# Gated cross attention and a quantized gated FFN on one core: seam between the two halves rewritten, out projections in two banks, weight passes spread over the steps, last two tiles' up products together

## The chip, the cores and the metric

One core of one Trainium2 chip. The metric is the device time of one execution in microseconds, the median over several runs.

## The reference

Inputs: `x` and `ctx` (8 x 256 x 512), attention weights with a latent width of 128, FFN weights w1, w2 (2048 x 512) and w3 (512 x 2048). For each of the 8 batches:

```
xn     = layernorm(x, axis=-1)                       # 256 rows of 512
theta  = theta_w @ ctx + theta_b                     # 128 x 512
phi    = phi_w @ xn + phi_b ;  g = g_w @ xn + g_b
p      = softmax(theta.T @ phi, axis=-1)             # 512 x 512
t_x    = g @ p.T                                     # 128 x 512
h      = relu((t_x - mean) * rsqrt(var + 1e-5) * gamma + beta)   # mean, var over all of t_x
x      = x + tanh(g_xattn) * (out_w @ h + out_b + ctx)
```

Then, row by row of all 2048 rows (16 tiles of 128 rows):

```
y      = layernorm(x)
bitlinear(a, w) = quant127(rmsnorm(a)) @ ternary(w).T      # per-row scale, one scale per weight
h      = silu(bitlinear(y, w1)) * bitlinear(y, w2)
x      = x + tanh(g_ffn) * bitlinear(h, w3)
```

## The kernel before, in words

The program is written engine by engine, each engine's instructions in a fixed order, with semaphores between them. It has two halves.

**Attention**, a loop of eight steps `i` (one batch each). On TensorE (PE) a step is `theta(i)`, `out_proj(i-3, 0)`, `phi(i)`, `mean_mm(i-2)`, `out_proj(i-3, 1)`, `g(i)`, then four rounds of `scores(i, c)`, `turn_p(i-1, c)` (transposes of the probabilities) and `values(i-1, c)`. So three batches are in flight. VectorE (DVE) takes the row maxima, the low halves of theta and phi, the layer norm of `t_x`, and adds each out projection to `x` (`add_out`, L675). ScalarE (ACT) copies products out of the banks, takes the exponentials and, in slots `slot(i, 0..6)` of each step, the **weight passes** of the FFN's ternary quantization: `weight_abs` (L435, `M` in the table) and `weight_sign` (L440, `S`), 128x1024 each, 8 of each kind per weight; a table `weight_work` says which pass stands in which slot. GpSimd (POOL) normalises the probabilities (L307), rounds the weights (L321) and takes all inverse roots (L283).

Both halves of an out projection go to one bank (`b_at`, bank 6), so `out_proj(i, 1)` waits until `add_out(i, 0)` has read it:

```
if 2 * i + o >= 1:
    pe.wait_ge(x2_ready, 2 * i + o)
```

**FFN**, a loop over 16 tiles `t`: `up(t, c)` for four column groups, each 4 matmuls of 128x512 with w1 and 4 with w2 into a pair of banks (L1023), SiLU on ACT (L501), `hmul` on DVE (L733) writes the hidden tile; `absmax` (L738) and `square` (L507) per half tile, `root_h` and `quant_h` on POOL (L374, L380) quantize it; a DMA transpose (L246) turns it; `down(t)` is 16 matmuls of 128x512 (L1042). PE's order is `up(t, 0..3)`, `down(t-2)`. Before a pair of tiles the input is prepared: `row_stats` and `prep_mean` (DVE), `center` (ACT), `prep_root` (POOL), `prep_max` and `prep_scale` (DVE), `prep_quant` (POOL), `turn_x` (a DMA transpose).

**The seam** is the stretch between the halves: the last batch's transposes and values, batches 5 to 7's layer norms and out projections, mixed by hand with tiles 0 and 1. There `prep_root(2)` stands on POOL between `root_h(1)` and `quant_h(1)`, and `row_stats(2)` on DVE in tile 2.

**The tail**: for the last tile the hidden tile is turned by 16 PE transposes (L1117) with copies on ACT and DVE (L583, L902), between `down(14)` and `down(15)`; before them PE runs `down(13)`, `down(14)`.

The start: 14 warm-up matmuls (L1048, two passes each), then `theta(0)`, once `ctx` of batch 0 has landed as one load.

Of the kernel before, what the change touches and what calls it, by code (L numbers as in the profile page):

```python
# [12 lines left out]
P = 128  # L13
# [21 lines left out]
def gated_cross_attention_bitffn(nc, x, ctx_in, pack_a, pack_b, pack_c, w1t, w2t, w3t, out):  # L35
# [22 lines left out]
    with ExitStack() as ctx:  # L58
# [33 lines left out]
        identb = sb("identb", [P, P], BF16)  # L92
# [35 lines left out]
        hT = [prob[:, k, 2:4].rearrange("p a t -> p (a t)").bitcast(BF16) for k in range(2)]  # L128
        xo = [stage[:, 4 * WP + k * T:4 * WP + (k + 1) * T] for k in range(2)]
# [3 lines left out]
        b_th, b_ph, b_g, b_tx, b_at, b_st = banks[0], banks[1], banks[2], banks[3], banks[6], banks[7]  # L133
# [14 lines left out]
        (pa_loaded, pb_loaded, pc_loaded, xa_loaded, ident_made, gates_ready, xvar_ready, xrstd_ready, xn_ready, cb_made,  # L148
# [4 lines left out]
            "pa_loaded", "pb_loaded", "pc_loaded", "xa_loaded", "ident_made", "gates_ready", "xvar_ready",  # L153
# [11 lines left out]
         tail_t_done, tail_T_ready) = [sem(n) for n in (  # L165
            "fvar_ready", "y_ready", "fr_ready", "fqs_ready", "xq_ready", "s12_ready",
            "up1_done", "up2_done", "sil_done", "hm_done", "sq_done", "hms_ready", "hr_ready", "qs_ready", "hq_ready",
            "dn_done", "xo_ready", "tail_a_ready", "tail_q_ready", "tail_t_done", "tail_T_ready")]
        tail_q1_ready, tail_T1_ready = sem("tail_q1_ready"), sem("tail_T1_ready")
# [14 lines left out]
        def _(sp):  # L184
# [19 lines left out]
            load_c(0)  # L204
# [51 lines left out]
            for t in range(1, NT):  # L256
# [12 lines left out]
        def _(pool):  # L269
# [882 lines left out]
```

## Time and profile before

| | us |
|---|---|
| median of 3 runs | 312.59 (312.37 to 313.79) |
| profiled execution, its own time | 312.92 |
| its span in the trace | 309.9 |
| PE busy | 298.2 (96%) |
| DVE / ACT / POOL busy | 240.3 / 196.2 / 195.9 |

The span runs from the first to the last instruction that the profile shows; 3.0 us of the execution's own time lie around it. Busy times of matmuls are modelled and overlap, so a busy PE can still be waiting a little. The start-to-start distance of two matmuls is the measure of what one costs.

### The profile page before, as it was taken

How to read it: one execution, taken by the hardware profiler on the slowest of the kernel's cores; microseconds unless marked ns; L12 is line 12 of the kernel's file. 1: busy time of each engine (PE TensorE's matmuls, PEld its weight loads, DVE VectorE, ACT ScalarE, POOL GpSimd, SP SyncE). 2: the span in 40 equal slices, each digit the busy share in tenths (PEclk: the TensorE clock that was granted, in tenths of full speed). 3: DMA queues.
4: the chain of work that ended last, by engine and by line, in shares of the span. 5: the costliest groups of instructions: out<-in, count | busy, mean ns of one | idle time of the engine just before them, and what ended most of it. 6: DMA issues, size and time to landing. Idle time of an engine off the chain costs nothing.

```text
span 309.9 us, 4392 instructions
## 1 busy us (share of the span) xinstructions
PE 298.2 (96%) x1345; PEld 161.4 (52%) x1362; DVE 240.3 (78%) x515; ACT 196.2 (63%) x343; POOL 195.9 (63%) x297
## 2 busy tenths in 40 slices
PE   8999999999999999999897999999999999999994
PEld 8766657575757665444343444444444444444451
DVE  3897878796969795877698798787976896768572
ACT  1498999789999837665953644736465546355430
POOL 3360959584949177683458878778686786655510
PEclk9999999999999999999999999999999999999999
DMA  7999953545020001010305433354234561642242
GB/s 261 418 414 413 384 211 139 203 135 205 0 69 0 0 6 30 1 36 1 68 2 102 103 63 91 85 122 117 53 83 102 71 119 52 138 102 48 54 102 102
DMA packets 50518, 36.45 MB, mean 118 GB/s; under 512 B 40896, under 2 KB 41024, under 8 KB 49472
## 3 DMA queue, kind: packets, MB, share of 16 engines
q1 hardware_dynamic: 50352, 36.05, 39.8%
q10 hardware_dynamic: 144, 0.13, 0.3%
q8 instruction: 10, 0.16, 0.2%
q14 instruction: 12, 0.10, 0.1%
HBM read 22.02 MB, written 4.19 MB: 85 GB/s over the span
## 4 chain that ended last, share of the span: by engine, by line
PE 70%; ACT 15%; DVE 9%; issue 4%; POOL 0%; DVEq 0%; ACTq 0%; POOLq 0%
PE bank L1023 30%; PE bank L1042 17%; ACT wq L435 5%; PE bank L969 4%; PE bank L951 4%; ACT prob L482 4%; PE bank L938 3%; PE bank L982 3%; PE bank L962 3%; ACT probT L478 2%; PE bank L1048 2%; PE bank L920 2%; DVE stage L733 1%; DVE x L675 1%; PE bank L930 1%
## 5 line engine op out<-in xcount | busy, mean ns | idle before, releaser
L1023 PE MATMUL bank<-wq,stage 128*128 128x512 bf16 x498 | 113.2, 379 | 3.4 <-DVE stage L733 2.7
L1023 PEld LDWEIGHTS bank<-wq,stage 128*128 128x128 bf16 x512 | 49.8, 98 | 65.9 <-DVE stage L733 5.2
L733 DVE SCALAR_TENSOR_TENSOR stage<-bank,s,stage 128x512 f32<-128x512 f32 x64 | 47.7, 745 | 30.7 <-PE bank L1023 20.6
L507 ACT ACTIVATE xn<-stage 128x1024 f32<-128x1024 f32 x32 | 33.8, 1057 | 47.8 <-DVE stage L733 47.8
L1042 PE MATMUL bank<-wq,prob 128*128 128x512 bf16 x253 | 57.4, 379 | 1.1 <-ACT prob L583 1.0
L501 ACT ACTIVATE stage<-bank,s 128x512 f32<-128x512 f32 x64 | 42.7, 680 | 21.3 <-PE bank L1023 19.2
L374 POOL TENSOR_SCALAR stage<-stage,hsc 128x1024 f32<-128x1024 f32 x30 | 33.4, 1122 | 21.5 <-DVE hsc L753 21.5
L307 POOL TENSOR_SCALAR prob<-prob,rsum 128x512 f32<-128x512 f32 x32 | 21.6, 693 | 35.8 <-DVE rsum L639 35.8
L1042 PEld LDWEIGHTS bank<-wq,prob 128*128 128x128 bf16 x256 | 25.0, 98 | 30.9 <-issue 0.9
L738 DVE TENSOR_REDUCE m<-stage 128x1 f32<-128x1024 f32 x32 | 38.9, 1216 | 0.8
L951 PE MATMUL bank<-ph,th 128*128 128x512 f32 x96 | 36.0, 488 | 0.0
L969 PE MATMUL bank<-probT,gs 128*128 128x512 f32 x64 | 32.9, 599 | 0.9 <-ACT probT L478 0.5
L380 POOL TENSOR_SCALAR prob<-stage 128x1024 bf16<-128x1024 f32 x30 | 30.9, 1046 | 0.0
L633 DVE TENSOR_REDUCE nmax<-bank 128x1 f32<-128x512 f32 x32 | 21.9, 690 | 10.8 <-PE bank L951 10.8
L321 POOL TENSOR_SCALAR stage<-stage,winv 128x1024 f32<-128x1024 f32 x24 | 29.2, 1230 | 0.4
L440 ACT ACTIVATE wq<-stage,neground 128x1024 bf16<-128x1024 f32 x24 | 26.9, 1150 | 0.0
L478 ACT COPY probT<-bank 128x512 f32<-128x512 f32 x32 | 18.7, 590 | 12.7 <-PE bank L962 12.7
L951 PEld LDWEIGHTS bank<-ph,th 128*128 128x128 f32 x96 | 17.5, 189 | 11.7 <-issue 10.0
L482 ACT ACTIVATE prob<-bank,nmax 128x512 f32<-128x512 f32 x32 | 22.3, 697 | 1.7 <-DVE nmax L633 1.7
L435 ACT ACTIVATE wq<-stage 128x1024 bf16<-128x1024 f32 x21 | 22.2, 1058 | 0.0
L962 PE MATMUL bank<-ident,prob 128*128 128x128 f32 x128 | 19.3, 275 | 0.0
L982 PE MATMUL bank<-hn,pc 128*128 128x512 f32 x32 | 17.3, 623 | 1.5 <-DVE x L675 1.1
(107 smaller groups left out, 421.7 us busy)
## 6 DMA issues: line engine op xcount, KB each, us to landing
c_sb<-ctx_in_dram SPq DMA_DIRECT2D x8, 512.0 KB, 3.9
stage<-w1t_dram SPq DMA_DIRECT2D x4, 1024.0 KB, 12.3
stage<-w2t_dram SPq DMA_DIRECT2D x4, 1024.0 KB, 14.7
stage<-w3t_dram SPq DMA_DIRECT2D x4, 1024.0 KB, 5.4
out_dram<-stage SPq DMA_DIRECT2D x16, 256.0 KB, 2.3
x<-x_dram SPq DMA_DIRECT2D x7, 512.0 KB, 11.7
pc<-pack_c_dram SPq DMA_DIRECT2D x1, 640.0 KB, 16.6
x<-x_dram SPq DMA_DIRECT2D x2, 256.0 KB, 3.6
```

The source lines that it names most:

```text
L374: link.inc(G.tensor_scalar(part, part, hsc[:, 5:6], ROUND, ALU.mult, ALU.add))
L380: G.tensor_scalar(hq[t % 2][:, lo:hi], h[:, lo:hi], -ROUND, 1.0, ALU.add, ALU.mult).then_inc(hq_ready, 1)
L435: A.activation(wq[:, at:at + WP], piece(k, p), ACT.Abs, accum_out=wsum[:, k, p:p + 1]).then_inc(wabs_done, 1)
L482: A.activation(prob[:, i % 2, c], b_sc(i, c)[:, :], ACT.Exp, bias=nmax[:, c:c + 1], accum_out=esum[:, c:c + 1]).then_inc(exp_done, 1)
L501: A.activation(sil[n % 3], up_banks(n)[0][:, :], ACT.Silu, scale=s12[:, u % 2, 0, k:k + 1]).then_inc(sil_done, 1)
L507: A.activation(junk, h_sb[t % 2][:, half * HF:(half + 1) * HF], ACT.Square, accum_out=ssq[:, half:half + 1]).then_inc(sq_done, 1)
L733: V.scalar_tensor_tensor(h_sb[k][:, c * 512:(c + 1) * 512], up_banks(n)[1][:, :], s12[:, u % 2, 1, k:k + 1], sil[n % 3], ALU.mult, ALU.mul ...
L738: link.inc(V.tensor_reduce(m2[:, half:half + 1], h_sb[t % 2][:, half * HF:(half + 1) * HF], AX_X, ALU.max, apply_absolute_value=True))
L951: last = mm(b_sc(i, c)[:, :], th[:, a, c * P:(c + 1) * P], ph[:, b], start=n == 0, stop=n == 2)
L969: last = mm(b_tx[:, :], gs[:, i % 2, c * P:(c + 1) * P], probT[:, c % 2], start=c == 0, stop=c == TC - 1)
L1023: last = mm(bank[:, :], turned[:, row:row + P], wq[:, at:at + 512], start=q == 0, stop=q == KI - 1)
L1042: last = mm(b_dn[t % 2][:, :], hT[t % 2][:, q * P:(q + 1) * P], wq[:, at:at + T], start=q == 0, stop=q == KF - 1)
```

## The change

What it does:

- **Start.** 9 warm-up matmuls for 14; batch 0's `ctx` loaded as two halves, waited for one by one by `theta(0)`; `phi(0)` waits for each half of `xn` by itself.
- **Weight passes.** The table has other entries (below): slot 4, before `g_copy`, is empty in steps 1 to 4, passes move to slots 5 and 6 and to later steps. In step 2 the weight's total, its scale and `mean_mm(0)` move behind `phi(2)` and `g(2)`.
- **Out projections.** The two halves go to two banks, `b_out(i, o)`; `out_proj(i, 1)` waits for `add_out(i-1, 1)` and no more for `add_out(i, 0)`. As bank 5 is also a transpose bank, `turn_p(i, 1)` waits for `add_out(i-2, 0)`.
- **Seam.** POOL normalises two of the last batch's four probability tiles, ACT the other two. `silu(0, 0)` stands between the copies of the last batch. Tile pair 2 is prepared inside the seam: `row_stats`, `prep_mean`, `center`, `prep_max` earlier, `prep_root(2)` behind `quant_h(0)`. The last weight signs, `hidden_scale`, `add_out`, `tx_gamma` and `out_proj(7, 1)` change places.
- **prep_scale.** Its operations on two columns become operations on one column each, and the scale that `prep_quant` waits for is written before the others.
- **Tail.** PE runs `up(14)`, `up(15)`, then `down(12)`, `down(13)`, `down(14)`, and tile 15's down product in two halves of 256 columns in two banks. Tile 15 is turned by DMA transposes, its last half tile is squared and maximised in two pieces, and its output is stored in two halves, the second from ACT's queue. The PE transposes and their copies are gone.

The diff, cut to its core:

```diff
+        def b_out(i, o):
+            if i < B - 2:
+                return (banks[5], banks[6])[o]
+            return ((banks[2], banks[6]), (banks[6], banks[2]))[i - (B - 2)][o]
...
-            load_c(0)
+            sp.dma_start(c_sb[:, 0, 0], c_v[0][:, 0]).then_inc(ca_loaded, 16)
+            sp.dma_start(c_sb[:, 0, 1], c_v[0][:, 1]).then_inc(c_loaded[0], 16)
...
-            normalise(B - 1)
+            normalise(B - 1, 2)
             tx_root(B - 2)
             rounds(2, 2, 4)
             prep_quant(1)
             rounds(2, 4, 8)
+            root_h(0)
             tx_root(B - 1)
-            root_h(0)
             quant_h(0)
+            prep_root(2)
             for t in range(2, NT):
                 root_h(t - 1)
-                if t == 2:
-                    prep_root(2)
                 quant_h(t - 1)
...
-                1: (None, (M, 0, 3), None, (M, 0, 4), (M, 0, 5), (M, 0, 6), (M, 0, 7)),
-                2: ((M, 1, 0), (M, 1, 1), (M, 1, 2), (M, 1, 3), (M, 1, 4), (M, 1, 5), (M, 1, 6)),
-                3: ((M, 1, 7), (S, 0, 0), (S, 0, 1), (S, 0, 2), (S, 0, 3), None, None),
-                4: ((S, 0, 4), (S, 0, 5), (S, 0, 6), (S, 0, 7), (M, 2, 0), (M, 2, 1), (M, 2, 2)),
-                5: ((S, 1, 0), (S, 1, 1), (S, 1, 2), (S, 1, 3), (M, 2, 3), (M, 2, 4), (M, 2, 5)),
-                6: ((S, 1, 4), (S, 1, 5), (M, 2, 6), (M, 2, 7), None, (S, 1, 6), (S, 1, 7)),
-                7: (None,) * 7,
+                1: (None, (M, 0, 3), None, (M, 0, 4), None, (M, 0, 5), (M, 0, 6)),
+                2: ((M, 0, 7), (M, 1, 0), (M, 1, 1), (M, 1, 2), None, (M, 1, 3), (M, 1, 4)),
+                3: ((M, 1, 5), (M, 1, 6), (M, 1, 7), (S, 0, 0), None, (S, 0, 1), (S, 0, 2)),
+                4: ((S, 0, 3), (S, 0, 4), (S, 0, 5), (S, 0, 6), None, (S, 0, 7), (M, 2, 0)),
+                5: ((S, 1, 0), (S, 1, 1), (S, 1, 2), (S, 1, 3), (M, 2, 1), (M, 2, 2), (M, 2, 3)),
+                6: ((S, 1, 4), (S, 1, 5), (M, 2, 4), (M, 2, 5), None, (M, 2, 6), (M, 2, 7)),
+                7: ((S, 1, 6), None, (S, 1, 7), None, None, None, None),
...
+            act.wait_ge(rsum_ready, B)
+            for c in (2, 3):
+                A.activation(prob[:, 1, c], prob[:, 1, c], ACT.Copy, scale=rsum[:, c:c + 1]).then_inc(pnorm_ready, 1)
             p_copy(B - 1, 0)
             p_copy(B - 1, 1)
+            silu(0, 0)
             p_copy(B - 1, 2)
...
-                link.inc(V.tensor_tensor(fsc[:, 8], fsc[:, 6], fsc[:, 7], ALU.mult))
-                link.wait(dve)
-                link.inc(V.tensor_scalar(fsc[:, 9], fsc[:, 8], QUANT_EPS, None, ALU.max))
+                for k in range(2):
+                    link.inc(V.tensor_scalar(fsc[:, 9, k:k + 1], fsc[:, 6, k:k + 1], fsc[:, 7, k:k + 1], QUANT_EPS,
+                                             ALU.mult, ALU.max))
...
             tx_norm(B - 2)
             prep_scale(1)
+            row_stats(2, 0)
+            row_stats(2, 1)
+            prep_mean(2)
             hmul(0, 1)
...
             def turn_p(i, c):
+                if c == 1 and i >= 2:
+                    pe.wait_ge(x2_ready, 2 * (i - 2) + 1)
...
-                if 2 * i + o >= 1:
-                    pe.wait_ge(x2_ready, 2 * i + o)
+                if o == 0 and i == B - 2:
+                    pe.wait_ge(exp_done, 4 * B)
+                elif i >= 1 and (o, i) != (1, B - 1):
+                    pe.wait_ge(x2_ready, 2 * i if o == 1 or i == B - 1 else 2 * i - 1)
...
-            for _ in range(14):
+            for _ in range(9):
                 mm(b_st[:, 0:P], avg[:, :], avg[:, :], start=True, stop=True)
...
             out_proj(B - 1, 0)
+            out_proj(B - 1, 1)
             for t in range(2, NT):
                 for c in range(FC):
                     up(t, c)
-                    if t == 2 and c == 0:
-                        out_proj(B - 1, 1)
-                down(t - 2)
-            down(NT - 2)
-            for half in range(2):
-                pe.wait_ge((tail_q_ready, tail_q1_ready)[half], 1)
...
-            down(NT - 1)
+                if t < NT - 2:
+                    down(t - 2)
+            for t in range(NT - 4, NT - 1):
+                down(t)
+            down_last()
```

ACT at the end of attention step 7 and the begin of the seam: `hn<-hn` is a relu, `stage<-x,fmv` the centering of tile pair 1, `prob,esum<-bank` an exponential, `probT<-bank` the copies of turned probabilities, `stage<-bank,s` a SiLU. Before:

```order
L482 ACTIVATE prob,esum<-bank,nmax 128x512
L501 ACT_TABLE_LOAD
L501 ACTIVATE stage<-bank,s 128x512
L440 ACTIVATE wq<-stage,neground 128x1024
L478 COPY probT<-bank 128x512 x4
L474 ACTIVATE hn<-hn 128x512
```

and now:

```order
L516 ACTIVATE prob,esum<-bank,nmax 128x512
L584 ACTIVATE prob<-prob,rsum 128x512 x2
L512 COPY probT<-bank 128x512 x2
L535 ACT_TABLE_LOAD
L535 ACTIVATE stage<-bank,s 128x512
L512 COPY probT<-bank 128x512 x2
L474 ACTIVATE wq<-stage,neground 128x1024
L508 ACTIVATE hn<-hn 128x512
```

Two normalising passes are new ahead of the first copies; the table load and the first SiLU have moved from before all four copies to between the second and the third; the weight sign has moved behind the copies.

POOL in the seam, from the root of tile 0's hidden tile (`hsc`) on; `fsc` is the preparation of tile pair 2, `stage<-stage,hsc` and `prob<-stage` are the two halves of `quant_h`. Before:

```order
L283 TENSOR_TENSOR hsc<-hsc,neghalf 128x1
L331 TENSOR_SCALAR fsc<-fmv 128x2
L283 TENSOR_TENSOR fsc<-fsc,neghalf 128x2
L335 TENSOR_TENSOR fsc<-fmv,fsc 128x2
L337 TENSOR_TENSOR fsc<-fsc 128x2
L339 TENSOR_SCALAR fsc<-fsc 128x2
L283 TENSOR_TENSOR fsc<-fsc,neghalf 128x2
L343 TENSOR_TENSOR fsc<-fsc 128x2
L374 TENSOR_SCALAR stage<-stage,hsc 128x1024 x2
```

and now:

```order
L415 TENSOR_SCALAR prob<-stage 128x1024 x2
L353 TENSOR_SCALAR fsc<-fmv 128x2
L305 TENSOR_TENSOR fsc<-fsc,neghalf 128x2
L357 TENSOR_TENSOR fsc<-fmv,fsc 128x2
L359 TENSOR_TENSOR fsc<-fsc 128x2
L361 TENSOR_SCALAR fsc<-fsc 128x2
L305 TENSOR_TENSOR fsc<-fsc,neghalf 128x2
L365 TENSOR_TENSOR fsc<-fsc 128x2
L380 TENSOR_TENSOR hsc<-ssq 128x1
L382 TENSOR_SCALAR hsc<-hsc 128x1
L305 TENSOR_TENSOR hsc<-hsc,neghalf 128x1
L409 TENSOR_SCALAR stage<-stage,hsc 128x1024 x2
```

The seven `fsc` operations stood between tile 1's root and its quantization; now they stand behind tile 0's quantization and ahead of tile 1's root.

PE in the tail, from the up products of tile 14 on. Before:

```order
L1023 MATMUL bank<-wq,stage 128x512 x32
L1042 MATMUL bank<-wq,prob 128x512 x16
L1023 MATMUL bank<-wq,stage 128x512 x32
L1042 MATMUL bank<-wq,prob 128x512 x32
L1117 MATMUL bank<-identb,prob 128x128 x16
L1042 MATMUL bank<-wq,prob 128x512 x16
```

and now:

```order
L1115 MATMUL bank<-wq,stage 128x512 x64
L1133 MATMUL bank<-wq,prob 128x512 x32
L1133 MATMUL bank<-wq,gs 128x512 x16
L1146 MATMUL bank<-wq,probT 128x256 x32
```

The 16 transposes are gone, and three down products instead of one and a half stand between the last up product and the last down product.

## Rows read from the trace of the kernel before

**Rows 1.** The page: busy times, and the shares of the chain that ended last.

```profile
PE 298.2 (96%) x1345; PEld 161.4 (52%) x1362; DVE 240.3 (78%) x515; ACT 196.2 (63%) x343; POOL 195.9 (63%) x297
...
PE 70%; ACT 15%; DVE 9%; issue 4%; POOL 0%; DVEq 0%; ACTq 0%; POOLq 0%
```

**Rows 2.** Windows, in us: length, busy of PE, PEld, DVE, ACT, POOL, PEclk, DMA, GB/s.

```profile
121.90:170.00 48.10, 43.91 (x186) 19.90 (x189) 38.00 (x82) 30.86 (x47) 30.48 (x44) 1.00 0.17 33
170.00:294.40 124.40, 123.77 (x566) 56.44 (x577) 97.53 (x208) 66.89 (x110) 89.11 (x138) 1.00 0.41 88
```

**Rows 3.** Chain of waits, one down product of the FFN: start, length, line.

```profile
190.86 3.45 PE bank L1042 x16
```

**Rows 4.** Timeline, the start: start, busy, instruction, [idle before it, ended by].

```profile
0.98 5.98 PE L1048 MATMUL bank<-avg 128*128 128x128 f32 x28 [0.98 <-POOL avg L272]
...
10.23 1.95 PE L938 MATMUL bank<-pb,xn 128*128 128x128 f32 x16
...
8.67 0.69 DVE L603 BATCH_NORM_STATS2 xst<-x 128x6 f32<-128x512 f32 x1 [0.98 <-DMA x<-x_dram]
```

**Rows 5.** Timeline, attention steps 1 and 2: an ACT weight pass, and PE where it waited.

```profile
20.13 1.04 ACT L435 ACTIVATE wq<-stage 128x1024 bf16<-128x1024 f32 x1
...
22.28 1.12 PE L969 MATMUL bank<-probT,gs 128*128 128x512 f32 x2 [0.46 <-ACT probT L478]
...
33.09 0.35 PE L990 MATMUL bank<-tsc,avg 128*128 128x1 f32 x2 [0.48 <-DVE winv L694]
```

**Rows 6.** Timeline of PE: mean and second out projection in steps 3, 4 and 7.

```profile
47.90 0.28 PE L990 MATMUL bank<-tsc,avg 128*128 128x1 f32 x2
48.32 1.12 PE L982 MATMUL bank<-hn,pc 128*128 128x512 f32 x2
...
63.72 0.28 PE L990 MATMUL bank<-tsc,avg 128*128 128x1 f32 x2
63.86 1.10 PE L982 MATMUL bank<-hn,pc 128*128 128x512 f32 x2
...
111.02 1.13 PE L982 MATMUL bank<-hn,pc 128*128 128x512 f32 x2 [0.29 <-DVE x L675]
```

**Rows 7.** Timeline of the seam: two of PE's waits, then POOL.

```profile
128.06 1.10 PE L969 MATMUL bank<-probT,gs 128*128 128x512 f32 x2 [0.42 <-DVE hn L665]
...
165.64 1.90 PE L1023 MATMUL bank<-wq,stage 128*128 128x512 bf16 x8 [1.10 <-DVE stage L733]
...
123.67 2.70 POOL L307 TENSOR_SCALAR prob<-prob,rsum 128x512 f32<-128x512 f32 x4 [1.16 <-DVE rsum L639]
...
157.75 0.19 POOL L331 TENSOR_SCALAR fsc<-fmv 128x2 f32<-128x2 f32 x1 [4.38 <-DVE fmv L704]
...
160.60 2.22 POOL L374 TENSOR_SCALAR stage<-stage,hsc 128x1024 f32<-128x1024 f32 x2
```

**Rows 8.** The page's groups: DVE's hidden product and half-tile maximum; mean in ns.

```profile
L733 DVE SCALAR_TENSOR_TENSOR stage<-bank,s,stage 128x512 f32<-128x512 f32 x64 | 47.7, 745 | 30.7 <-PE bank L1023 20.6
...
L738 DVE TENSOR_REDUCE m<-stage 128x1 f32<-128x1024 f32 x32 | 38.9, 1216 | 0.8
```

**Rows 9.** DVE beside POOL: tx_norm in the seam; two lines' ns min/median/max.

```profile
129.74 1.19 DVE L670 SCALAR_TENSOR_TENSOR hn<-hn,tsc,pc 128x512 f32<-128x512 f32 x1
...
L717 DVE TENSOR_SCALAR fsc<-fsc x8: 169/170/1083, 111.2 to 264.6; 128x2 f32<-128x2 f32 x8
...
L751 DVE TENSOR_SCALAR dq<-hsc,fk x16: 194/196/198, 145.4 to 298.5; 128x1 f32<-128x1 f32 x16
```

**Rows 10.** The tail: chain of waits; last, line L246 (DMA transposes).

```profile
301.37 0.46 PE bank L1117 x8
...
303.22 3.41 PE bank L1042 x15
...
306.66 0.75 DVE stage L759
...
DMA to landing us min/median/max: 3.1/3.2/4.9
```

More of the change, by code:

```diff
@@ L578, in _ @@
             act.wait_ge(tail_a_ready, 1)
-            for half in range(1):
-                act.wait_ge(hT_loaded[1][half], 16 * (NU - 1))
+            act.wait_ge(hT_loaded[1][0], 16 * (NU - 1))
             A.activation(hq[1][:, 0:HF], h_sb[1][:, 0:HF], ACT.Identity, bias=neground[:, 0:1]).then_inc(tail_q_ready, 1)
-            act.wait_ge(tail_t_done, 1)
-            A.copy(hT[1][:, 0:HF], banks[0][:, :].bitcast(BF16)).then_inc(tail_T_ready, 1)
+            act.wait_ge(xo_ready, NT + 1)
+            act.dma_start(out_v[:, NT - 1, T // 2:T], xo[1][:, T // 2:T]).then_inc(last_stored, 16)
         @block.vector
@@ L855, in _ @@
             hmul(1, 1)
+            hidden_scale(0)
             tx_norm(B - 1)
-            hidden_scale(0)
+            prep_max(2, 0)
+            prep_max(2, 1)
             hmul(1, 2)
@@ L877, in _ @@
                 absmax(t, 0)
+                if t == 2:
+                    prep_scale(2)
                 if odd:
@@ L887, in _ @@
                     prep_scale(t // 2 + 1)
-                hmul(t, 3)
-                absmax(t, 1)
-                hidden_max(t)
+                if t == NT - 1:
+                    absmax_last(0)
+                    hmul(t, 3)
+                    absmax_last(1)
+                else:
+                    hmul(t, 3)
+                    absmax(t, 1)
+                    hidden_max(t)
             hidden_scale(NT - 1)
@@ L899, in _ @@
             V.tensor_scalar(hq[1][:, HF:], h[:, HF:], -ROUND, 1.0, ALU.add, ALU.mult).then_inc(tail_q1_ready, 1)
+            down(NT - 4)
             down(NT - 3)
-            dve.wait_ge(tail_t_done, 2)
-            V.tensor_copy(hT[1][:, HF:], banks[1][:, :].bitcast(BF16)).then_inc(tail_T1_ready, 1)
             down(NT - 2)
-            down(NT - 1)
+            dve.wait_ge(xo_free[1], 16 * (NU - 1))
+            for part, bank in enumerate(b_last):
+                lo, hi = part * T // 2, (part + 1) * T // 2
+                dve.wait_ge(dn_done, NT + part)
+                V.scalar_tensor_tensor(xo[1][:, lo:hi], bank[:, 0:T // 2], dq[:, 3:4], x_tile(NT - 1)[:, lo:hi], ALU.mult, ALU.add)\
+                    .then_inc(xo_ready, 1)
         @block.tensor
@@ L1060, in _ @@
                 g(i)
+                if i == 2:
+                    mean_mm(0, 0)
                 if i >= 1:
@@ L1108, in _ @@
                     up(t, c)
-                    if t == 2 and c == 0:
-                        out_proj(B - 1, 1)
-                down(t - 2)
-            down(NT - 2)
-            for half in range(2):
-                pe.wait_ge((tail_q_ready, tail_q1_ready)[half], 1)
-                for n in range(KF // 2):
-                    at = (half * KF // 2 + n) * P
-                    last = tr(banks[half][:, :].bitcast(BF16)[:, n * P:(n + 1) * P], hq[1][:, at:at + P], identb[:, :])
-                last.then_inc(tail_t_done, 1)
-            down(NT - 1)
+                if t < NT - 2:
+                    down(t - 2)
+            for t in range(NT - 4, NT - 1):
+                down(t)
+            down_last()
 def kernel(**inputs):
```

212 lines of the change are left out of this document (139 added, 73 removed).

## The prediction

> **What bounds the kernel now.** I first read busy times and the chain that ended last: PE is busy 96% of the span and carries 70% of the chain; ACT has 15%, DVE 9%, nobody else counts [rows 1]. So only what shortens PE's own list or lets it wait less can move the end. Next, windows by stage: from 170 to 294.4 us PE is busy 123.8 of 124.4 us, in the seam (121.9 to 170) only 43.9 of 48.1 [rows 2]. The FFN's steady part has nothing to give; the seam, the start, the attention steps and the tail have.
>
> The price of PE's work: a down product is 16 matmuls in 3.45 us [rows 3], 0.216 each; an up group (8) is 1.73 us, a tile's up products 6.9 us. An f32 pass of 128 columns costs 0.112 (16 in 1.95 with the drain [rows 4]), so an out projection or a value product (two passes of 512) costs some 0.86.
>
> **The change part by part.** Times are the profiled execution's.
>
> *Start.* The 28 warm-up passes take 5.98 us, 0.21 each, against 0.12 for the same shape at 10.23 [rows 4]: they ran at the lower of TensorE's two clock levels (1.2 GHz), the later ones at 2.4. Ten passes fewer free PE 2.1 us earlier, at about 4.8. But then PE waits for the half loads of `ctx`, and DVE, which must make the low halves of theta and phi before `scores(0, 0)`, still waits until 8.67 for batch 1's `x` [rows 4], whose load is now issued behind one more load. Behind it stand two statistics, two low halves: that puts the scores 0.2 us earlier. Bounds: 0.4 lost (one issue on SP later), 0.5 gained. I take **0.2**.
>
> *Weight passes.* In step 1 ACT did two passes of 1.04 between phi and `g_copy`; `values(0, 0)` waited for the probability copy, 0.46 shown as idle [rows 5], some 0.7 from start to start. With slot 4 empty the copy comes 1.04 earlier: **0.65**. Bounds 0.46 and 0.9. In step 2 `mean_mm(0)` waited for the weight's scale, 0.48 shown [rows 5], 0.7 from start to start; now it stands behind `g(2)`, 1.8 us later, and the scale is long there. ACT's `g_copy` also comes a pass earlier there. I take **0.85**, bounds 0.48 and 1.1. Does ACT pay it back later? A step's fixed work is about ten passes of a 128x512 tile at 0.5 to 0.7, 6.8 us, and at most seven weight passes of 1.04 are 7.3: 14.1 of the 15.3 us of a step. Steps 3 to 6 still fit; cost nothing while PE is the slower one.
>
> *Out projections in two banks.* In step 4 the second projection starts 0.14 behind the mean, in step 3 0.42 behind: 0.28 waited for `add_out` [rows 6]. Steps 5 and 6 look like step 3. In step 7 the trace shows 0.29 idle, and by the same measure 0.4 in all. Sum 3 x 0.28 + 0.4 = **1.25**. It is late next at `scores(i, 0)`, which needs the low half of phi: about 1 us ahead in steps 3, 5, 6, hardly 0.1 in step 7. The new wait of `turn_p(i, 1)` is for an `add_out` that DVE finishes 4 us before: nothing. Bounds 0.8 and 1.3.
>
> *Seam.* PE's work from `out_proj(5, 0)` to `down(1)` is 16 up groups (27.6), one down (3.45), six out projections and four value products (8.6), 16 transposes (1.8), four small products (0.6): 42.1 of the 48.1 us [rows 2], so **6.0 us are waits**. The largest that is shown, 1.10 before 165.64 [rows 7], and the waits around it come from tile 1's quantization, which on POOL stood behind `prep_root(2)`: POOL waited 4.38 us for DVE's statistics of pair 2, then took 2.85 us for the roots before it began at 160.60 [rows 7]. With the statistics taken some 24 us earlier, the roots follow at once on `quant_h(0)` and `quant_h(1)` begins near 154. The statistics still cost DVE 1.5 us, now where PE waits for DVE. At the seam's begin POOL's four normalising passes take 2.70 [rows 7]; two on each of POOL and ACT take half, and `turn_p(7, 0)` no longer waits. I laid the four lists beside each other with the durations of the trace. Three waits remain: 0.3 before `values(7, 2)`, as a table load and a SiLU now stand between ACT's copies; 0.4 before `up(1, 1)`, where DVE has 11 passes of the size of `hmul` (0.745 [rows 8]), one half-tile maximum (1.216 [rows 8]) and 16 small ones, some 11.1 us, between `hmul(0, 0)` and `add_out(6, 1)`; and small ones, 0.4 together. That is 1.1.
>
> To this comes DVE against POOL. In the seam `tx_norm(6)` took 1.19 us beside a POOL rounding pass, 0.45 more than the 0.745 of its size [rows 8, 9]; a two-column `prep_scale` operation took up to 1.083 us instead of 0.17 beside POOL's passes, while a one-column operation (L751) never took over 0.198 in 16 times [rows 9]. Both `tx_norm` of the seam now fall beside POOL passes of 1.1 us, each on a path that PE waits for: I add 0.6 and 0.7 us. The waits left are then 2.4 us, the gain **3.6**. Bounds: nothing added, 4.9; DVE's list 1.5 us longer, 2.1. The Trainium skill ("SBUF — State Buffer", section "SBUF: two separate sides") says that DVE and GpSimd share one pair of ports as an exclusive lock, also for DVE operations with two SBUF inputs, so that the loser waits for the whole instruction. The rows at 129.74 and L717 agree. By that rule, which speaks against putting `tx_norm(7)` beside `quant_h(0)`, the seam gives 3.6; without it it would give 4.9.
>
> *Tail.* Now PE ends `down(14)` at 301.37, starts the last down product at 303.22 and ends near 306.66; a 0.75 DVE pass and the store follow to 309.9 [rows 10]. The 1.85 us between are the 16 transposes and the copies. In the new order `up(14)` and `up(15)` run from 277.2 to 291.0, since hidden products keep pace: per up group of 1.73 DVE has one `hmul` and half a maximum, 1.3 us. Then three downs, 10.35, end at 301.35, exactly as before. Tile 15's last product is done near 293, its quantization near 297 by the durations of today's tail shifted by 3.5 us minus the pieces; the two DMA transposes land 3.2 us after issue [rows 10], at 300.2 and 301.5, the second needed only at 302.2. So `down_last` starts at 301.4: **1.85** gained. It costs 32 matmuls of 256 columns, 3.45 if they cost half of 512. The output is written in halves: half a DVE pass and half a store behind the end, **0.45**. Bounds: transposes 1.7 us late (landing 4.9 [rows 10]) or a 256-column matmul costing 0.13, 1.0; nothing late and a faster store, 2.6.
>
> Sum: 0.2 + 0.65 + 0.85 + 1.25 + 3.6 + 2.3 = 8.85 us. Against the profiled execution's 312.92 that is 304.1; the median 312.59 lies 0.3 lower, which gives **303.8**. With all lower bounds the gain is 4.4 us, with all upper ones 11.3.
>
> **The rivals.** (1) *DVE becomes the bound of the seam.* It is busy 38 of 48.1 us there [rows 2], and the seam shrinks to some 44 with 1.5 us of statistics placed in its tightest part. If hidden products follow its list through tile 2 as well, the seam gives 1.0 instead of 3.6: 306.4. For it: nearly no slack from `tx_norm(6)` to tile 1's last maximum. Against: the three prices above already hold the known delays. (2) *The last tile's transposes come late*, behind the quantization chain of root, scale, round and issue of 1.3 us each on SP: 1.5 us of the tail are lost, 305.3. Against: a us of slack on the first half. (3) *The two banks don't help*: the wait moves to the low half of phi in each step; 1.25 less, 305.0. Against: a us of distance there. (4) *The clock rises later.* PE has a gap before `theta(0)` that it had not before; if the level of 1.2 GHz lasts until batch 0's projections are through, scores start 0.6 later than now instead of 0.2 earlier, 304.6. The Trainium skill ("TensorE: Matmul & The Clock Gate", section "Why this matters for your kernels") asks for TensorE to be kept busy at the start without a break and by that rule this rival would hold; no row here shows such a start with a gap. (5) *Slower:* ACT falls behind PE in attention. It decides if its seven passes and fixed work exceed the 15.3 us of a step; today they make 14.1. If the passes stretched from 1.04 to 1.6 us beside the other engines, each of five steps would be 2.7 us longer, 13.5 in all: 317.3. Against: no pass in the trace did. (6) *Nothing moves*: gains are taken back before the FFN's steady part; it would need a new wait there, which 123.8 busy of 124.4 us makes unlikely: 312.
>
> **How the numbers follow.** Forecast 0.60; DVE-bound seam 0.15; late transposes 0.08; banks 0.06; clock 0.05; slower 0.03; nothing 0.03. The time is the likeliest case, 303.8. The range goes down to 301.3, where all upper bounds meet, and up to 307.0, past the DVE-bound case and short of all lower bounds together (308.2). About 0.5% of the time, 1.6 us, is what a measurement of this kernel tells from no change: faster 0.94, same 0.03, slower 0.03.
>
> **What would show it.** Right: PE's wait at `values(0, 0)` and behind `mean_mm(0)` gone; second out projections 0.14 behind the mean; `down(1)` beginning some 6.5 us earlier than 170; POOL's roots of pair 2 ahead of tile 1's root without waiting; `down_last` following `down(14)` with no gap. Wrong: a PE wait of over 1 us for DVE at `up(1, 1)`, `up(2, *)` or for the last DMA transposes, or seven-pass steps of more than 15.4 us.

## The result, and the profile after

The changed kernel takes 303.87 us (median of 4 runs, 302.98 to 304.85) against 312.68 us before: ratio 0.971, 95% interval 0.967 to 0.975. The forecast was 303.8. Its profiled execution took 304.05 us with a span of 302.3; before, 312.92 with 309.9.

The page of the changed kernel, busy times and the chain that ended last [rows 1]:

```profile
PE 294.6 (97%) x1336; PEld 159.8 (53%) x1352; DVE 240.7 (80%) x541; ACT 196.9 (65%) x346; POOL 194.1 (64%) x294
...
PE 83%; DVE 6%; DMA 3%; issue 3%; SPq 2%; ACT 1%; POOLq 0%; DVEq 0%; POOL 0%
```

ACT's share of the chain fell from 15% to 1%. PE is busy 3.6 us less (ten warm-up passes and 16 transposes are gone) and idle some 4 us less; the other engines' work is the same within 2 us. The windows by stage, the seam first, then the steady part [rows 2]:

```profile
121.90:163.50 41.60, 40.82 (x177) 19.20 (x179) 36.27 (x87) 31.38 (x49) 29.88 (x43) 1.00 0.26 39
163.50:294.70 131.20, 130.57 (x597) 59.37 (x607) 104.80 (x233) 68.14 (x113) 88.95 (x140) 1.00 0.42 90
```

These windows do not hold the same work as those before: the first begins 2.4 us inside the seam, and the second holds the three down products behind `up(15)`. Over the same work, from `out_proj(5, 0)` to `down(1)`, the seam takes 44.02 us with PE idle for 0.8; before, 48.08 with 4.2 idle. The four longest of PE's waits, in us in total, times, longest:

```profile
PE bank L1153 <- POOL avg L296: 1.0, 1, 1.0
PE bank L1007 <- DMA c_sb<-ctx_in_dram: 0.6, 1, 0.6
PE bank L1039 <- DVE ph L679: 0.5, 1, 0.5
PE bank L1115 <- DVE x L726: 0.4, 1, 0.4
```

The timeline of the changed kernel has the places that the prediction named: the start, step 1 (`values(0, 0)` at 21.75, no wait), step 7 (mean and second out projection), the seam and POOL's roots of pair 2, `down(1)`, then the tail. A wait too short to be shown as idle, as ahead of `values(7, 2)` at 127.71, is read from one start to the next.

```profile
0.98 4.01 PE L1153 MATMUL bank<-avg 128*128 128x128 f32 x18 [0.98 <-POOL avg L296]
5.62 1.95 PE L1007 MATMUL bank<-c_sb,pa 128*128 128x512 f32 x4 [0.63 <-DMA c_sb<-ctx_in_dram]
9.13 0.69 DVE L654 BATCH_NORM_STATS2 xst<-x 128x6 f32<-128x512 f32 x1 [1.98 <-DMA x<-x_dram]
...
21.75 1.02 PE L1059 MATMUL bank<-probT,gs 128*128 128x512 f32 x2
...
108.49 0.28 PE L1082 MATMUL bank<-tsc,avg 128*128 128x1 f32 x2
108.63 1.10 PE L1074 MATMUL bank<-hn,pc 128*128 128x512 f32 x2
...
127.01 0.60 PE L1052 MATMUL bank<-ident,prob 128*128 128x128 f32 x4
127.71 1.98 PE L1059 MATMUL bank<-probT,gs 128*128 128x512 f32 x4
...
128.17 0.56 POOL L305 TENSOR_TENSOR tsc<-tsc,neghalf 128x1 f32<-128x1 f32 x1 [5.54 <-DVE tsc L710]
128.72 2.65 POOL L343 TENSOR_SCALAR stage<-stage,winv 128x1024 f32<-128x1024 f32 x2
129.19 1.18 DVE L721 SCALAR_TENSOR_TENSOR hn<-hn,tsc,pc 128x512 f32<-128x512 f32 x1
...
139.20 1.02 PE L1115 MATMUL bank<-wq,stage 128*128 128x512 bf16 x4 [0.37 <-DVE x L726]
...
142.91 0.75 DVE L721 SCALAR_TENSOR_TENSOR hn<-hn,tsc,pc 128x512 f32<-128x512 f32 x1
143.15 1.50 POOL L409 TENSOR_SCALAR stage<-stage,hsc 128x1024 f32<-128x1024 f32 x1 [1.66 <-DVE hsc L819]
...
147.85 0.19 POOL L353 TENSOR_SCALAR fsc<-fmv 128x2 f32<-128x2 f32 x1
152.59 2.22 POOL L409 TENSOR_SCALAR stage<-stage,hsc 128x1024 f32<-128x1024 f32 x2 [0.81 <-DVE hsc L819]
...
163.53 3.62 PE L1133 MATMUL bank<-wq,prob 128*128 128x512 bf16 x15
...
294.75 3.91 PE L1146 MATMUL bank<-wq,probT 128*128 128x256 bf16 x32
299.12 0.88 DVE L987 SCALAR_TENSOR_TENSOR stage<-bank,dq,x 128x256 f32<-128x256 f32 x2 [1.83 <-DMA out_dram<-stage]
```

The roots of pair 2 wait for nothing, `down(1)` begins 6.45 us earlier, and tile 1's scaling starts at 152.59 in place of 160.60 [rows 7]. DVE's normalising pass of step 6 takes 1.18 us beside POOL's pass of 2.65. The last output pass has a wait that the kernel before had not.

Where the time went is read from six stretches between starts on PE: to `theta(1)`, to `theta(3)`, to `theta(7)`, to `down(1)`, to the end of `down(14)` (the start of what follows it on PE), to the end of the span. For all kernels of this study, the length of each stretch in us in the profiled execution, and the median of the times:

| kernel | to theta(1) | theta(3) | theta(7) | down(1) | end of down(14) | span's end | median us (runs) |
|---|---|---|---|---|---|---|---|
| before | 14.87 | 28.73 | 62.34 | 64.04 | 131.22 | 8.70 | 312.68 (4) |
| changed | 14.96 | 27.37 | 61.65 | 59.55 | 131.22 | 7.55 | 303.87 (4) |
| e1_own_buffer | 14.60 | 27.36 | 61.69 | 59.55 | 131.25 | 6.65 | 303.00 (4) |
| e2_old_tail | 14.52 | 27.35 | 61.68 | 59.55 | 131.22 | 8.68 | 306.52 (4) |
| e3_pair2_late | 14.57 | 27.36 | 61.66 | 59.43 | 132.98 | 7.40 | 305.30 (1) |
| e4_one_bank | 14.53 | 27.36 | 62.99 | 60.42 | 131.23 | 6.67 | 305.01 (1) |
| e5_rounds_early | 14.48 | 27.37 | 61.65 | 59.09 | 131.27 | 7.44 | 303.16 (1) |
| e6_silu_first | 15.19 | 27.36 | 61.69 | 58.74 | 131.27 | 7.35 | 303.40 (1) |
| e7_theta_first | 14.68 | 27.37 | 61.66 | 59.52 | 131.24 | 7.23 | 303.57 (1) |
| e8_two_columns | 14.14 | 27.36 | 61.66 | 59.76 | 131.23 | 7.45 | 303.48 (1) |
| e9_changed_again | 14.27 | 27.37 | 61.66 | 59.54 | 131.26 | 7.40 | 303.72 (4) |
| e10_old_tail_again | 14.36 | 27.37 | 61.67 | 59.55 | 131.23 | 8.72 | 305.02 (5) |
| e11_best | 14.47 | 28.27 | 61.66 | 58.73 | 131.25 | 6.72 | 302.86 (5) |
| e12_old_passes | 14.50 | 28.82 | 61.68 | 59.54 | 131.28 | 7.28 | 305.17 (5) |

Where nothing was changed, the four middle stretches repeat to 0.06 us. The first wanders by 1.05 us (14.14 to 15.19) over eleven kernels with the same start, and the last by up to 0.9: a single run's time does not resolve 0.5 us here, a middle stretch does. Between the two profiled executions the change gained -0.09, 1.36, 0.69, 4.49, 0.00 and 1.15, together 7.60 us of span. This pair is not a typical one: the median span is 310.3 over the 19 executions of the kernel before that list one, and 301.9 over the changed kernel's eight, 8.4 us less.

### The profile page after: what moved, and what is told of

Its sections match the earlier page's. It is cut to its first block, busy times and chain, and to the rows that moved or that the text cites. A ratio compares the mean times of both kernels' runs of the same rounds, so it can differ in the third digit from the quotient of the medians.

```text
span 302.3 us, 4409 instructions
## 1 busy us (share of the span) xinstructions
PE 294.6 (97%) x1336; PEld 159.8 (53%) x1352; DVE 240.7 (80%) x541; ACT 196.9 (65%) x346; POOL 194.1 (64%) x294
## 4 chain that ended last, share of the span: by engine, by line
PE 83%; DVE 6%; DMA 3%; issue 3%; SPq 2%; ACT 1%; POOLq 0%; DVEq 0%; POOL 0%
PE bank L1115 34%; PE bank L1133 14%; PE bank L1059 8%; PE bank L1039 7%; PE bank L1052 4%; PE bank L1074 4%; PE bank L1026 4%; PE bank L1018 3%; PE bank L1007 3%; DMA x<-x_dram 2%; DMA out_dram<-stage 1%; DVE stage L788 1%; SPq L266 1%; DVE x L726 0%; DVE xst L654 0%
## 5 line engine op out<-in xcount | busy, mean ns | idle before, releaser
L543 ACT ACTIVATE xn<-stage 128x1024 f32<-128x1024 f32 x31 | 32.8, 1057 | 44.8 <-DVE stage L788 44.8
L1133 PE MATMUL bank<-wq,prob 128*128 128x512 bf16 x221 | 50.3, 379 | 0.2
L329 POOL TENSOR_SCALAR prob<-prob,rsum 128x512 f32<-128x512 f32 x30 | 20.2, 695 | 34.3 <-DVE rsum L690 34.3
L793 DVE TENSOR_REDUCE m<-stage 128x1 f32<-128x1024 f32 x31 | 37.7, 1215 | 0.8
L1133 PEld LDWEIGHTS bank<-wq,prob 128*128 128x128 bf16 x224 | 21.9, 98 | 26.4
L1052 PEld LDWEIGHTS bank<-ident,prob 128*128 128x128 f32 x128 | 15.7, 146 | 3.6 <-issue 1.3
```

The source lines that it names most:

```text
L543: A.activation(junk, h_sb[t % 2][:, half * HF:(half + 1) * HF], ACT.Square, accum_out=ssq[:, half:half + 1]).then_inc(sq_done, 1)
L793: link.inc(V.tensor_reduce(m2[:, half:half + 1], h_sb[t % 2][:, half * HF:(half + 1) * HF], AX_X, ALU.max, apply_absolute_value=True))
L1052: last = tr(b_pt[c % 2][:, tc * P:(tc + 1) * P], prob[:, i % 2, tc, c * P:(c + 1) * P], ident[:, :])
L1133: last = mm(b_down(t)[:, :], turned_h(t)[:, q * P:(q + 1) * P], wq[:, at:at + T], start=q == 0, stop=q == KF - 1)
```

## The experiments

**Tail: the last store's buffer.**

```diff
-            dve.wait_ge(xo_free[1], 16 * (NU - 1))
-                V.scalar_tensor_tensor(xo[1][:, lo:hi], bank[:, 0:T // 2], ...
+                V.scalar_tensor_tensor(sil[1][:, lo:hi], bank[:, 0:T // 2], ...
```

> The last tile's product is written into a buffer that nothing else uses by then (a silu buffer) in place of xo[1], and the wait for the store of tile 13 is gone. Theory (the tail is now bound by a store): in the changed kernel DVE's last output pass waited 1.83 us for the store of tile 13, which took 4.41 us; without it the pass follows PE's last product, the chain of waits no longer holds that store, and the span is 0.9 us shorter than the changed kernel's 302.3. Rival (the two last stores and the work outside the span set the end anyway): the pass comes earlier but the time stays within 0.3 us.

The end of e1's timeline:

```profile
294.45 3.93 PE L1145 MATMUL bank<-wq,probT 128*128 128x256 bf16 x32
295.58 2.52 PEld L1145 LDWEIGHTS bank<-wq,probT 128*128 128x128 bf16 x24 [0.38 <-DMA probT<-prob]
...
296.92 0.48 DVE L986 SCALAR_TENSOR_TENSOR stage<-bank,dq,x 128x256 f32<-128x256 f32 x1
298.41 0.48 DVE L986 SCALAR_TENSOR_TENSOR stage<-bank,dq,x 128x256 f32<-128x256 f32 x1 [1.02 <-PE bank L1145]
```

The first half is written 1.5 us before PE ends, the second right behind it, both without a wait for a store. The tail is 6.65 us, 0.90 shorter than the changed kernel's: the theory holds. The wait is not there in every execution, though: in e4, which still had it, the store had landed and the tail took 6.67. In the eight other traces with this buffer the last pass waited 1.5 to 1.8 us and the tail took 7.23 to 7.55. So the buffer costs 0 to 0.9 us; the medians differ by 0.7 to 0.9.

**Tail: the old one put back** (transposes on PE, the down products of tiles 12 and 13 between the last up products), twice.

```diff
-            for t in range(NT - 4, NT - 1):
-                down(t)
-            down_last()
+            down(NT - 2)
+            for half in range(2):
...
+                    last = tr(banks[half][:, :].bitcast(BF16)[:, n * P:(n + 1) * P], hq[1][:, at:at + P], identb[:, :])
+            down(NT - 1)
```

> The tail of the kernel before in the changed kernel: the last tile's transposes on PE, the down projections of tiles 12 and 13 where they were; all else as changed. Theory (what the two traces show as the tail's share of the span): the stretch from the end of down(14) to the end of the span goes from 7.55 us back to 8.55, and the span is 1.0 us longer than the changed kernel's 302.3. Rival A (the forecast's 2.3 us was right and the rest lies outside the span): the run is 1.8 to 2.3 us longer than 303.9, the time outside the span going from 1.8 back to 3.0 us. Rival B: the tail gave nothing, within 0.3 us.

> The tail of the kernel before in the changed kernel, again, since its trace said 1.1 us (8.68 us from the end of down(14) to the end, against 7.55) and its four runs said 2.4 by the median of their spans. If the trace's tail is the truth: 1.0 to 1.3 us above the changed kernel beside it, 304.9 to 305.2. If the forecast's 2.3 us was right and its trace was a lucky run: 2.0 to 2.6 us above, 306 to 306.5.

The traces gave 8.68 and 8.72 us, 1.1 to 1.3 above the changed kernel. The first set of runs had a median of 306.52, the second 305.02, and only the second ran beside the changed kernel (303.72): 1.3 us. So the traces and the paired runs say 1.1 to 1.3 us, not 2.3. All nine runs with the old tail (median 305.6) against all eight of the changed kernel (303.7) would say 1.9; both traces are of the fastest run of their set, so where the slower ones lost more is not shown. The time outside the span stayed at 1.8 to 2.2 us with the old tail, as in the changed kernel (1.75 to 1.9) and not as before (2.1 to 3.3, mostly 2.2), so the tail is not why that fell.

**Seam: pair 2 prepared late.**

```diff
             quant_h(0)
-            prep_root(2)
...
             prep_scale(1)
-            row_stats(2, 0)
-            row_stats(2, 1)
-            prep_mean(2)
             hmul(0, 1)
...
                 hidden_scale(t - 1)
+                if t == 2:
+                    row_stats(2, 0)
+                    row_stats(2, 1)
+                    prep_mean(2)
                 hmul(t, 1)
```

> The third input tile is prepared where the kernel before did it, in tile 2 of the feed-forward network, with the seam's other order kept as changed. Theory (the seam gained by having the preparation ahead of tile 2): up(2,*) and up(3,*) wait for DVE again as in the kernel before, and 3 to 4 of the 4.06 us that the seam gained are lost: 307 to 308 us. Rival (the order and the split of the normalising passes in the seam did it): less than 1 us lost, near 304.5.

e3's timeline of PE:

```profile
173.37 1.90 PE L1114 MATMUL bank<-wq,stage 128*128 128x512 bf16 x8 [1.33 <-DVE stage L790]
```

The stretch up to `down(1)` is as short as in the changed kernel, the wait comes one tile later, and 1.76 us are lost (1.4 by the time of this one run, 305.30 against 303.87). Neither theory hit: with the rest in place the early preparation is worth 1.6 to 1.8 of the seam's 4.06 us. The remaining 2.3 come with the rest of the new order: half of the normalising on ACT, other places of the signs, additions and the SiLU, and 0.2 of the one-column form (e8 below). No run took these apart, so how much of it the shared normalising is worth is not shown.

**Banks and weight passes.**

```diff
-                return (banks[5], banks[6])[o]
+                return banks[6]
```

That is e4, with the old wait for the addition; e12 puts the old table of weight passes back and changes nothing else:

```diff
-                1: (None, (M, 0, 3), None, (M, 0, 4), None, (M, 0, 5), (M, 0, 6)),
+                1: (None, (M, 0, 3), None, (M, 0, 4), (M, 0, 5), (M, 0, 6), (M, 0, 7)),
...
```

> Both halves of the out projection in bank 6 again, with the waits that this needs; all else as changed. Theory (two banks were worth their forecast): the second out projection starts 0.42 us behind the mean and not 0.14, in steps 3, 5 and 6 and with 0.4 us in step 7, so 1.1 to 1.3 us longer: 305.0. Rival (what PE waits for there is DVE anyway, a step later): within 0.3 us of 303.9.

> ScalarE's weight passes by the table of the kernel before; two banks and all else as changed. Theory: steps 1 and 2 lose the 1.36 us that they gained; steps 3 to 6, which took 62.34 us before, 61.65 changed and 62.99 with one bank and the new table, then take 61.0 if the two edits add, for with one bank the new table costs 0.65 us there; in sum 0.7 to 1.4 us above the changed kernel. Rival (two banks hide the place of the passes in steps 3 to 6, so that PE is bound by its own work at about 15.3 us a step): 61.3 to 61.7, and all of 1.4 us lost, 305.3.

PE's waits in e4, then in e12:

```profile
PE bank L1074 <- DVE x L726: 1.3, 4, 0.5
```

```profile
PE bank L1059 <- ACT probT L512: 0.9, 2, 0.5
```

With one bank, 2.2 us are lost: 1.34 in steps 3 to 6, 0.87 from step 7 on, more than either theory said. (The time of this one run, 305.01, is only 1.1 above the changed kernel's, and as the theory had it by luck: in this execution the start and the tail, which were not touched, were 1.3 us shorter.) With the old table, steps 1 and 2 lose 1.45 and steps 3 to 6 nothing (61.68 against 61.65): the rival of e12. Of the 1.45, 0.65 fall in step 2, although `mean_mm(0)` still stands behind `g(2)` in e12: PE then waits for ACT's copy ahead of `values(1, 0)` instead (0.40 at 36.83). Moving the mean with the old table gains nothing: 14.83 us for the step, 14.81 before.

The table and the banks do not add: steps 3 to 6 took 62.34 with the old table and one bank, 62.99 with the new table and one bank, and 61.65 or 61.68 with two banks and either table. Passes spread into those steps make the first out addition late; two banks hide that. The spreading pays in steps 1 and 2 alone, the banks from step 3 on.

**Seam: POOL's rounding first, the SiLU first, the two-column form.**

```diff
-            tx_root(B - 2)
             rounds(2, 2, 4)
+            tx_root(B - 2)
```

is e5, and e6 is

```diff
+            silu(0, 0)
             p_copy(B - 1, 0)
             p_copy(B - 1, 1)
-            silu(0, 0)
```

In e8 the input scale's one-column operations are written as one of two columns again:

```diff
-                for k in range(2):
-                    link.inc(V.tensor_scalar(fsc[:, 9, k:k + 1], ...
+                link.inc(V.tensor_scalar(fsc[:, 9], fsc[:, 8], QUANT_EPS, None, ALU.max))
```

> POOL rounds the second half of a weight slab (2.65 us, L343) in the 5.5 us in which it idles ahead of its roots for step 6, not behind them. Theory (DVE's normalising pass of step 6 took 1.18 us and not 0.75 because it ran beside that POOL pass): the pass takes 0.75 us, the 0.37 us wait of up(1,1) goes, and the feed-forward network starts 0.4 us earlier: 303.5. Rival (the pass is slow for its operands): it takes 1.18 us again and nothing moves.

> ScalarE does the first SiLU, and with it the load of its table (1.28 us), before the two copies of step 7. Theory (PE's 0.26 us wait ahead of values(7,2) and part of DVE's lateness at up(1,1) hang on that load): values(7,0) starts 0.2 to 0.35 us later, the wait ahead of values(7,2) is gone, the product hmul(0,0) on DVE comes over 2 us earlier and the wait of up(1,1) goes: 0.6 us faster in sum, 303.3. Rival (the load is only moved to where PE waits for the copy): values(7,0) loses over 0.8 us, time 304.2 or more.

> The small operations of the input scale again as one of two columns each instead of two of one column. Theory (the one-column form was made so that they don't block on POOL's pass): beside POOL's 2.65 us pass in the seam one of them is delayed by about 1 us, and up(1,1) starts up to 1 us later: 304.3 to 304.9. Rival (both forms are the same to DVE): within 0.2 us of the changed kernel, or slightly faster for fewer instructions.

e5, timeline, the normalising pass and the up group that had waited 0.37:

```profile
128.70 0.74 DVE L721 SCALAR_TENSOR_TENSOR hn<-hn,tsc,pc 128x512 f32<-128x512 f32 x1
...
138.26 2.10 PE L1115 MATMUL bank<-wq,stage 128*128 128x512 bf16 x9
```

0.74 with POOL idle beside it, 1.18 with POOL in its pass, on the same operands: the delay is POOL's. The stretch is 0.46 us shorter, as expected. e6, timeline:

```profile
122.83 1.28 ACT L535 ACT_TABLE_LOAD   x1
125.34 1.12 PE L1059 MATMUL bank<-probT,gs 128*128 128x512 f32 x2 [0.45 <-ACT probT L512]
...
132.10 0.75 DVE L788 SCALAR_TENSOR_TENSOR stage<-bank,s,stage 128x512 f32<-128x512 f32 x1 [0.97 <-ACT stage L535]
```

PE waits 0.45 us at `values(7, 0)`, which comes 0.33 later behind `theta(7)` than in the changed kernel, and all the same the stretch is 0.81 shorter, as the theory had it; DVE now waits where it was late. e8 keeps its up(1, 1) wait of 0.37 and loses 0.21. The lines of the operation by ns min/median/max, first in e8, two columns, then in the changed kernel, one:

```profile
L768 DVE TENSOR_SCALAR fsc<-fsc x8: 168/168/994, 108.4 to 257.5; 128x2 f32<-128x2 f32 x8
```

```profile
L767 DVE TENSOR_SCALAR fsc<-fsc x16: 198/202/214, 108.9 to 258.1; 128x1 f32<-128x1 f32 x16
```

So the delay is there with two columns (0.90 us at 129.66 in the seam, in place of 0.17) and absent with one, as the theory had it. But the one-column form has nine operations for six, and these take most of it back: the form is worth 0.2 us, the size that the rival named, not 1.

**Start, and all together.** e7 has DVE take theta's low half ahead of the next input's statistics; e11 joins e1, e5 and e6 with a step 0 in which both low halves come ahead of the second half of the statistics, and the first row maximum ahead of `x_norm(1)`. The order of DVE's step 0 in e11, written out for this step:

```diff
+                low_part(0, th, b_th, 0, th_ready, thl_ready)
                 x_stats(1, 0)
-                low_part(0, th, b_th, 0, th_ready, thl_ready)
+                low_part(0, ph, b_ph, 1, ph_ready, phl_ready)
                 x_stats(1, 1)
-                low_part(0, ph, b_ph, 1, ph_ready, phl_ready)
-                x_norm(1)
                 row_max(0, 0)
+                x_norm(1)
```

e7 has the first and third of these lines alone.

> In step 0 DVE takes the low part of theta before the statistics of the next input. Theory (scores(0,0) waits 0.53 us for DVE's high part of phi, which stands behind those statistics): scores(0,0) starts 0.5 us earlier, at 11.6 us, and all behind it too, unless the next input's centring then comes late: 303.4. Rival (step 0 is bound by the landing of the second input at about 9.1 us): theta(1) starts at 14.9 us as before and nothing is gained.

> Four things together: the last tile's own output buffer; POOL's rounding ahead of its roots; the first SiLU ahead of the copies of step 7; and in step 0 DVE takes the low parts of theta and of phi before the second half of the next input's statistics, which puts the scores right behind the Gram products. The parts measured 0.9 (tail), 0.46 and 0.78 us (from theta(1) to down(1)); the start should give the 0.27 to 0.5 us that scores(0,0) waited for DVE. If they add: 2.4 us below the changed kernel beside it, 301.5. If the two in the seam overlap (both remove the same lateness of DVE at up(1,1)): 1.9 us, 302.0. Rival: what they free is taken back by the next wait (the silu then waits for PE's values in the seam), under 1 us.

> The changed kernel once more, beside the next three on one chip. Its runs so far spread from 302.98 to 304.85 us. Expected: 303.9 again, with the spread coming from the start (theta(1) began between 14.14 and 15.19 us in eight kernels whose start is the same) and from the landing of the last stores; the stretch from down(1) to the end of down(14) takes 131.22 us again.

e7, timeline of DVE:

```profile
8.83 0.75 DVE L679 SCALAR_TENSOR_TENSOR th<-bank,pa,th 128x512 fp32r<-128x512 f32 x1 [1.56 <-ACT th L496]
9.50 1.27 DVE L654 BATCH_NORM_STATS2 xst<-x 128x6 f32<-128x512 f32 x2
10.81 0.25 DVE L659 BATCH_NORM_AGGREGATE xmv<-xst 128x2 f32<-128x6 f32 x2
10.97 0.72 DVE L679 SCALAR_TENSOR_TENSOR ph<-bank,pa,ph 128x512 fp32r<-128x512 f32 x1
```

Both statistics still stood ahead of phi's low half, so the scores began at 11.84, within the scatter of the others (11.30 to 12.37): no gain can be seen. Between the theories it decides little; the operation that mattered was not moved. e11 moved it. Its timeline:

```profile
10.75 0.75 DVE L679 SCALAR_TENSOR_TENSOR ph<-bank,pa,ph 128x512 fp32r<-128x512 f32 x1 [0.43 <-ACT ph L500]
11.65 2.98 PE L1044 MATMUL bank<-ph,th 128*128 128x512 f32 x12
13.54 1.00 DVE L669 TENSOR_SCALAR xn<-x,xmv,xrs 128x512 f32<-128x512 f32 x2 [0.23 <-POOL xrs L305]
15.18 0.69 ACT L516 ACTIVATE prob<-bank,nmax 128x512 f32<-128x512 f32 x1 [1.06 <-DVE nmax L684]
```

The scores no longer wait for DVE. But the input's normalisation now stands between the first and the second row maximum, ACT waits 1.06 us before its second exponential, and in step 1 PE waits 0.72 for the normalised probabilities: that stretch is 28.27, 0.90 longer. The two moves in the seam do not add either: 0.81 together, as much as e6's alone. So e11 gained 0.81 and some 0.7 in the tail, gave 0.90 back, and comes to 302.86 us, 0.9 below the changed kernel beside it. Both of its forecasts, 301.5 and 302.0, were missed. That changed kernel, e9, took 303.72 us and 131.26 from `down(1)` to the end of `down(14)`, as expected. The ratios to before, 0.969 [0.967, 0.972] and 0.972 [0.970, 0.973], overlap a little. By the stretches the same kernel without its change of step 0 would be near 302.0; it was not run.

## Why the prediction was right, term by term

The time was right to 0.1 us, and that closely only by luck. Between the profiled executions 8.85 us were forecast and 7.60 found in the span; the rest came from outside it, for which the sum had no term. Up to `down(1)` the sum held (6.55 forecast, 6.45 found), in part because the errors of its terms cancel; in the tail it did not.

- *Start*, 0.2: **-0.09**. The load of batch 1's `x` came 0.46 later (statistics at 9.13, not 8.67 [rows 4]), and what stands behind it gave 0.37 back: the scores begin 3.0 us behind the start of those statistics in all eleven traces with this start, and 3.4 before. With the median of the eleven, 14.52, the gain is 0.35; of the start before there is one trace only.
- *Weight passes*, 0.65 + 0.85 = 1.50: **1.36**, of it 0.73 in step 1 and 0.63 in step 2; e12, with the old table, lost 1.45. The cause given for step 2, the wait for the scale, was not enough by itself, as e12 shows. That the passes cost nothing later held only with the two banks.
- *Two banks*, 1.25: **1.12** in place (0.69 in steps 3 to 6: 0.30, 0.01, 0.27 and 0.11 us, the last where 0.28 was forecast; 0.43 in step 7, where `out_proj(5, 0)` came at 119.51 in place of 121.90 [rows 2] and `theta(7)` 1.96 earlier). Taking them back alone costs 2.2: the term was priced as if the new table were not there. Second out projections stand 0.14 behind the mean, as forecast.
- *Seam*, 3.6: **4.06**, what is left of that stretch's 4.49. By the prediction's 42.1 us of work, 1.9 us of waits are left; it had 2.4. The waits at `values(7, 2)` and `up(1, 1)` stand where it placed them, 0.26 from start to start and 0.37 shown. But the 0.4 charged for `up(1, 1)` and the 0.6 for `tx_norm(6)` are one wait: `tx_norm(6)` was delayed by 0.44, and e5, without that delay, lost the wait too and gained 0.46 in all. The 0.7 charged for `tx_norm(7)` was not paid: it took 0.75, since it began 0.24 us ahead of POOL's pass, which took 1.50 itself. So 1.2 us were charged too much, and the small waits, charged 0.4, must be some 0.8 longer (a remainder, not seen one by one). What the prediction had as the largest cause, pair 2's statistics ahead of tile 1's root, is the 1.6 to 1.8 us of e3; the other half of the term was right in size, but no run shows its causes.
- *Tail*, 2.3: **1.15**, the failed step: a wait that the sum put at nothing without a reason. The last output pass waits for the store of tile 13, which frees its buffer, which SP issues only behind the last transposes and which landed 4.41 us after its issue; that costs 0.9. With its own buffer (e1) the tail gives 2.05, and there the terms can be read. The PE transposes and copies that are gone took 1.81 in e2 (1.85 forecast). From the first last down product to the pass that reads its last bank it is 3.96 us in e1 and 3.65 in e2: the half-width products cost half, as assumed, and 0.3 is the wait for the second transposing DMA, which landed at 295.5. From that pass to the end of the span it is 2.7 in place of 3.2, some 0.5 less (0.45 forecast). (Before, two down products stood behind the last up product, not one and a half as said above.)
- *Outside the span* lay 1.75 to 1.9 us in the changed kernel's runs, 3.0 in the profiled execution before and mostly 2.2 in its others. In the comparison of profiled executions that 1.2 us made up for the tail. In the medians it is 0.4 (2.2 against 1.8), and the other 0.8 us are in spans that the profiled pair does not show: 310.3 to 301.9 in place of 309.9 to 302.3. Why the time outside fell by 0.4 is open.

The rivals: (1) DVE is busy 37.2 of 44.0 us in the seam and only one wait of PE for it is shown, 0.37; it is not the bound. (2) The transposes came 0.3 late, not 1.5. (3) The banks help. (4) The clock rose in time: 18 warm-up passes in 4.01 us are 0.22 each, yet `theta(0)`, behind a gap of 0.63, ran its four f32 products in 1.95 us, as later ones do (1.88). The two levels are read from these durations; the profile's clock column says 1.00 for both stretches, before and after. The Trainium skill ("TensorE: Matmul & The Clock Gate", section "Why this matters for your kernels") asks for TensorE to be kept busy continuously at the start. The trace agrees: the passes from 0.98 to 4.99 us stand back to back, and the gap behind them cost nothing. (5) Steps 3 to 6 took 15.3 to 15.5 us, the one with seven passes 15.33; ACT kept up.

The lock of the Trainium skill ("SBUF — State Buffer", section "SBUF: two separate sides") says that of DVE and GpSimd the one that starts first has the shared ports for its whole instruction. The trace agrees on both sides: at 129.19 DVE came second and took 1.18 us, at 142.91 it came first and POOL took 1.50. The forecast used the rule for both passes, and missed that in the second DVE comes first.

## What to carry to other kernels

When a product, a transposition or a store is taken off the end, list the buffers that the new last instruction writes and ask which transfer frees each: here one buffer took back 0.9 of 2.05 us. Edits that hide the same wait, or of which one hides what the other makes late, must be priced as a pair; here two banks were worth 0.7 us with one table and 1.3 with the other in the same four steps. Two charges on one path can be one wait: `up(1, 1)` was charged 1.0 us twice over and paid 0.46. And compare stretches between fixed instructions, not single times, where the start wanders by a microsecond.

## What the runs showed of the hardware

- A small DVE operation took up to 0.994 us on two columns, beside a POOL pass, and never over 0.215 on one column, in 64 operations (e8 against the changed kernel). For the same product of scales, `s<-fsc,fk`, it is 0.897 against 0.205 at most.
- A DVE pass of 0.75 us that began 0.24 us before POOL's wasn't delayed; POOL's took 1.50 us, where two such passes took 2.22.
- The store of tile 13, the second one behind two transposing DMAs on SP's queue, landed 4.41 us after its issue; the median of all such stores is 2.3. In ten of eleven traces with this order the slowest store there took 4.1 to 4.4 us, in one (e4) 2.4; what decides it is not shown.
- The landing of batch 1's input moved the start of step 1 by 1.05 us over eleven executions with the same start: DVE's first statistics on it began at 8.29 to 9.36 us, and the scores 3.0 us behind that each time.
